# Sixteen row tiles per step from GpSimd in the second layer, in place of fourteen or fifteen from GpSimd and one or two picked by TensorE

## The reference: what is computed

```python
e_feat = jnp.concatenate([x[rol], x[col], edge_attr], axis=-1)
h = jax.nn.relu(e_feat @ W1 + b1)
v = h @ W2 + b2
x_cand = jax.ops.segment_max(v, col, num_segments=num_nodes)
```

```python
x = h[src]; y = h[dst]
c = w_comp[etype]
xb = jnp.einsum('ei,bio->ebo', x, weight)
msg = jnp.einsum('eb,ebo->eo', c, xb)
a = jnp.tanh(jax.nn.relu(jnp.sum(x_hat * y_hat, axis=-1) / scale))
nei = jax.ops.segment_sum(a[:, None] * msg, dst, num_segments=N)
```

## Time and profile before

| | |
|---|---|
| time, median of 3 runs | 4428.0 us (4425.21 to 4429.86) |
| span of the profiled execution | 5626.5 us |
| PE, DVE, ACT, POOL busy in it | 4271.1, 2911.1, 742.0, 3153.8 us |
| granted TensorE clock in it, mean | 0.886 |
| layer 0's steps (copy L885, 104 times) | first at 361.1, last at 2437.9 us |
| layer 1's steps (copy L946, 104 times) | first at 2854.7, last at 5457.4 us |
| DMA bytes | 561.10 MB, mean 100 GB/s |

### The profile page before, as it was taken

How to read it: one execution, slowest core, us unless ns; L and a number is a source line. 1 busy time by engine, 2 the same in 40 slices (tenths; PEclk the granted TensorE clock), 3 DMA queues, 4 the chain that set the end, 5 groups by cost and what they waited for, 6 DMA issues and landing times.

```text
span 5626.5 us, 60937 instructions
## 1 busy us (share of the span) xinstructions
PE 4271.1 (76%) x21573; PEld 1819.3 (32%) x21573; DVE 2911.1 (52%) x5217; ACT 742.0 (13%) x1303; POOL 3153.8 (56%) x3284
## 2 busy tenths in 40 slices
PE   5878888888888777722868888888888878888751
PEld 2434444444444333311323333333323333333211
DVE  5733333333333332334456666666666666666653
ACT  3401111111111100110011111111111111111111
POOL 6556666666666555445455555555555555555535
PEclk8989999999999898965979999999999999999975
DMA  6023323333332222220155556555656555555531
GB/s 262 20 63 86 80 73 81 79 81 77 80 79 73 71 66 66 72 57 25 32 119 132 130 131 134 132 138 130 134 127 139 128 132 127 139 128 135 125 78 30
DMA packets 515150, 561.10 MB, mean 100 GB/s; under 512 B 174276, under 2 KB 371201, under 8 KB 512673
## 3 DMA queue, kind: packets, MB, share of 16 engines
q1 hardware_dynamic: 364960, 392.61, 29.0%
q0 software_dynamic: 104960, 55.52, 6.7%
q10 hardware_dynamic: 44928, 109.07, 5.1%
HBM read 377.15 MB, written 179.68 MB: 99 GB/s over the span
## 4 chain that ended last, share of the span: by engine, by line
PE 41%; another core or an unknown queue 29%; DVE 12%; issue 10%; ACT 3%; DMA 1%; ACTq 1%; DVEq 0%; SPq 0%; POOL 0%; POOLq 0%
PE psum L1471 9%; PE psum L1633 7%; PE psum L1556 6%; PE psum L1565 5%; DVE late L1303 3%; PE psum L1507 3%; PE psum L1517 1%; PE psum L1457 1%; PE psum L1713 1%; PE psum L1447 1%; DVE scan L1316 1%; PE psum L1584 1%; PE psum L1641 1%; PE psum L1596 1%
## 5 line engine op out<-in xcount | busy, mean ns | idle before, releaser
L740 POOL DMA_INDIRECT rows_in<-h_dram,src_idx x1494 | 1428.0, 956 | 1218.2 <-ACT early L941 522.9
L740 POOL DMA_INDIRECT rows_in<-in_x_dram,src_idx x1392 | 1331.1, 956 | 866.0 <-issue 294.7
L1303 DVE TENSOR_TENSOR late<-late,psum 128x512 f32<-128x512 f32 x1664 | 1085.5, 681 | 791.1 <-PE psum L1556 399.7
L1471 PE MATMUL psum<-early,late 128*128 128x448 bf16 x5712 | 1212.6, 367 | 91.6 <-issue 78.3
L1556 PE MATMUL psum<-comp,sel 128*128 128x512 bf16 x1664 | 635.6, 412 | 461.9 <-DVE late L1303 401.4
L1471 PEld LDWEIGHTS psum<-early,late 128*128 128x128 bf16 x5712 | 560.0, 101 | 799.4 <-issue 357.2
L1633 PE MATMUL psum<-x,rows_in 128*128 128x448 bf16 x1988 | 572.1, 358 | 0.0
L1099 DVE TENSOR_TENSOR late<-psum,lane_hot 128x448 f32<-128x448 f32 x272 | 169.3, 622 | 659.9 <-issue 317.2
L1565 PE MATMUL psum<-late,basis 128*32 128x512 f32 x3328 | 493.5, 668 | 0.0
L1556 PEld LDWEIGHTS psum<-comp,sel 128*128 128x128 bf16 x1664 | 160.2, 100 | 969.5 <-DVE late L1303 687.2
L1208 DVE TENSOR_TENSOR_SCAN scan<-fresh,scan,psum 128x512 f32<-128x512 bf16 x103 | 131.8, 1280 | 491.9 <-remote 245.5
(11 more groups left out here) (157 smaller groups left out, 4445.3 us busy)
## 6 DMA issues: line engine op xcount, KB each, us to landing
late<-xs_dram SPq DMA_DIRECT2D x416, 256.0 KB
sp_in<-spread SPq DMA_DIRECT2D x208, 256.0 KB, 2.6
late<-type_dram SPq DMA_DIRECT2D x104, 512.0 KB
sum_rows<-early ACTq DMA_DIRECT2D x104, 512.0 KB
spread<-late SPq DMA_DIRECT2D x16, 1664.0 KB
ea<-in_edge_t SPq DMA_DIRECT2D x104, 256.0 KB
keep<-keep_dram SPq DMA_DIRECT2D x832, 32.0 KB
max_rows<-out ACTq DMA_DIRECT2D x104, 256.0 KB
```

The lines of the kernel that those rows point to most:

```text
L740: pool.indirect_dma_start(out=out, out_offset=None, in_=table, in_offset=bass.IndirectOffsetOnAxis(ap=index, axis=0), engine_sem=pool_issu ...
L1303: dve.tensor_tensor(prod[:, n % G_BUFS, :], x4[:, s.slot(2), g, :], bank[C_BANK[n]][:, :], ALU.mult).then_inc(prod_ready, 1)
L1471: last_ = pe.matmul(hot_bank[tile_slot(s, t)], class_hot[s.slot(2)][:, c, HOT - hot_tiles(s) + t, :], x_parts[:, c, q, :], start=c == 0 an ...
```

## The change

From step 2 of layer 1 on GpSimd gathers all sixteen tiles. `hot1_count` and its tables are gone, and with them TensorE's `hot_rows`, VectorE's `find_lane`, `mask_hot` and `add_hot`, SyncE's `hot_save` in layer 0 and `hot_load` in layer 1 with the DRAM tensor between, and every wait on their semaphores: in `build_hot` (layer 0), ahead of the score sum, `relate`, `source_turn` and the copy of the source rows (layer 1). TensorE's picks in layer 0 and for the first two steps of layer 1 stay as they are.

```diff
-FIRST_HOT1 = 6
-LAST_HOT1 = STEPS - 2
-HOTS1 = (1, 2)
-PIECES1 = {1: (0, 0, 6, 11, 11, 16, 21), 2: (0, 7, 14, 21, 28, 35, 42)}
...
-    return SLOTS - (hot1_count(n) if n >= EARLY1 else min(EARLY_TILES - SLOTS * n, SLOTS))
+    return SLOTS if n >= EARLY1 else SLOTS - min(EARLY_TILES - SLOTS * n, SLOTS)
...
             for n in range(PRE):
-                hot_save(Step(PRE, 0, n))
...
-                if hot(s.plus(2)):
-                    hot_save(s.plus(2))
...
-            for u in range(2):
-                sp.wait_ge(hot_saved[u], 16 * (STEPS // 2))
...
                 keep_load(1, s)
-                if has_pick(s):
-                    hot_load(s)
...
-                for k in range(SLOTS - hot1_count(s.at)):
+                for k in range(SLOTS):
                     if k in (BURST, 2 * BURST, 3 * BURST) and s.at >= 3:
...
-                    wait_count(dve, s, hot_saved[u], s.earlier(2) * 16)
...
-                for t in range(hot1_count(ahead.at)):
-                    mask_hot(ahead, t)
-                product(s, 0)
-                for t in range(hot1_count(ahead.at)):
-                    add_hot(ahead, t)
-                products(s, 1, 5)
+                products(s, 0, 5)
...
-                if has_pick(later):
-                    find_lane(later)
...
-                if has_pick(s):
-                    wait_count(pe, s, hot1_ready, hot1_before(s.at + 1))
...
                 coefs(s, 8, 10)
-                if pick:
-                    hot_rows(later, 0)
                 messages(s, 0)
                 coef(s, 10)
                 messages(s, 1)
-                if pick:
-                    hot_rows(later, 1)
...
                 coef(s, 15)
-                if pick:
-                    hot_rows(later, 5)
                 messages(s, 2)
```

More of the change, by code:

```diff
@@ L204, in build @@
         early_dram = dram("early_dram", [EARLY_TILES * P], fp16)
-        hot_dram = dram("hot_dram", [STEPS * P, max(HOTS1) * CLASSES * P], bf16)
         ident = sb("ident", [P, P])
@@ L282, in build @@
         xs = rows_in[:, 2 * SLOTS * F:2 * SLOTS * F + 2 * LEN].rearrange("p (u n) -> p u n", u=2)
[L283 to L289, removed]
         ea = sb("ea", [P, 2, LEN])
@@ L342, in build @@
         h_low = part(NODE_COLS * F // 2).bitcast(bf16).rearrange("p (c n) -> p c n", c=CLASSES)
-        picks1 = part(max(HOTS1) * PICK * F).rearrange("p (t f h) -> p t f h", f=F, h=PICK)
         h_high = x[:, :, :].rearrange("p t f -> p (t f)").bitcast(bf16).rearrange(
@@ L364, in build @@
         hot_bank = [bank[6 + u][:, 0:PICK * F] for u in range(2)]
-        hot_bank1 = [bank[b][:, 0:PICK * F] for b in (1, 5)]
-        def hot1_bank(s, t):
-            return hot_bank1[t - hot1_count(s.at)]
         lane_v = lane[:, 0:HOT_COLS].rearrange("p (s t) -> p s t", t=HOT)
@@ L457, in build @@
         lane_ready = sem("lane_ready")
-        hot_saved = [sem(f"hot_saved{u}") for u in range(2)]
         h_parts_ready = sem("h_parts_ready")
[L460 to L464, removed]
         early_loaded = [sem(f"early_loaded{u}") for u in range(2)]
@@ L496, in pe_picks @@
             return hot(s) and hot_tiles(s) > 0
-        def has_pick(s):
-            return hot1_count(s.at) > 0
         def gathered1(s, use):
@@ L537, in build @@
         class_v = class_dram.rearrange("(s n) -> s n", s=STEPS)
-        hot_v = hot_dram.rearrange("(s p) n -> s p n", p=P)
         h_nodes = h_dram.rearrange("(p t) f -> p t f", p=P)
@@ L598, in class_load @@
                              class_v[s.at].partition_broadcast(P)).then_inc(classes_in[s.slot(2)], 16)
[L600 to L611, removed]
             def keep_load(n, s):
@@ L937, in src_copy @@
                     wait_count(act, s, gathered[1][s.slot(2)], gathered1(s, 1))
-                if has_pick(s):
-                    wait_count(act, s, hot1_ready, hot1_before(s.at + 1))
                 wait_out(act, s, stored[1])
@@ L1317, in sum_scan @@
                                        ALU.mult, ALU.add).then_inc(scanned[1], 1)
[L1320 to L1339, removed]
             def products(s, a, b):
@@ L1572, in score_sum @@
                 wait_step(pe, s, score_ready)
-                if hot1_count(s.at + 1) == len(hot_bank1):
-                    wait_count(pe, s, hot1_read, hot1_before(s.at + 1) + 1)
                 pe.matmul(bank[1][:, :], ones_blk[:, :], score, start=True, stop=True).then_inc(sum_done, 1)
@@ L1591, in relate @@
                 wait_step(pe, s, query_ready, lag=1)
-                if has_pick(s):
-                    wait_count(pe, s, hot1_read, hot1_before(s.at + 1))
                 for q in range(PARTS):
@@ L1617, in source_turn @@
                 last_.then_inc(x_turned[1], 1)
[L1619 to L1636, removed]
             def find_key(s):
@@ L1647, in step1 @@
             def step1(s):
-                behind, ahead, later = s.plus(-1), s.plus(1), s.plus(2)
-                more, pick = ahead.exists(), has_pick(later)
+                behind, ahead = s.plus(-1), s.plus(1)
+                more = ahead.exists()
                 turns_last = s.known and s.at == STEPS - 2
@@ L1683, in step1 @@
                     find_key(ahead)
-                if pick:
-                    hot_rows(later, 2)
                 coef(s, 13)
-                if pick:
-                    hot_rows(later, 3)
                 coef(s, 14)
-                if pick:
-                    hot_rows(later, 4)
                 coef(s, 15)
-                if pick:
-                    hot_rows(later, 5)
                 messages(s, 2)
```

## The result

| kernel | median us | step of layer 1, us |
|---|---|---|
| before | 4427.3 (4425.21 to 4429.86) | 19.75 |
| changed | 4474.6 (4474.09 to 4482.6) | 20.27 |

The changed kernel is slower by 1.2%: the ratio is 1.0116, with a 95% interval of 1.0103 to 1.0128. The forecast was 4565, with a range of 4420 to 4640: the sign and the new bound were right, the old bound and the size were not, +47 us for +137.

The account below looks back on a forecast made before the run. GpSimd was taken to bound both layers' steps, or very nearly: +178 us for 142 more gathers, -40 us for a loss that goes, everything else nothing, so +138 on 4428.0 us, forecast 4565 us, range 4420 to 4640 us.

Parts of the forecast that it names:

- rival A: Layer 1's steps: GpSimd not quite the bound, real steps 19.3 us before, only +82 us, 4510 us; chance 0.18.
- TensorE's 17.7 us: TensorE's work alone in a layer 1 step before: 12.2 us of chain pieces plus 5.5 us for 1.39 picked tiles.
- The budget of 290 us: Timed 4428.0 us less GpSimd's 4138: 290 left, 246 outside the loops, some 45 for waits in both layers' steps.
- The loss that goes with the change: Layer 1's steps before: GpSimd and TensorE holding each other up, at most 0.8 us a step, 82 us; taken as 40.
- 142 x 1.256 = +178 us: GpSimd in layer 1: 142 more gathered tiles at 1.256 us each, if GpSimd is the bound all along.
- Nothing for VectorE, saves, loads: VectorE's 175 us of masks and sums, 104 saves and 96 loads go: nothing, at most 2.6 us for the transfers.
- The ring, 16.0 to 18.6 us: Source rows' way through DRAM, turn to product 0 to next turn, in layer 1: 16.0 to 18.6 us, below GpSimd's 20.1.
- B: Gap between GpSimd's gathers belongs, at least partly, to the recording: changed kernel faster, -133 us, 4295 us; chance 0.12.
- C: GpSimd still waits for ScalarE's copy or coef 3 each step: steps 20.4 to 21.4 us, 4630 to 4740; chance 0.07.
- D: TensorE's granted clock falls to 0.50 at 61% busy: its step 24.4 us, 440 us above the forecast; chance 0.03.
- The forecast of a span near 5200 us: Changed kernel's profiled span: about 5200 us, 340 to 530 less than the recorded 5626.5, steps at 20.1 to 22 us.
- one sign of being right: In the changed kernel's profile, TensorE idle ahead of the turn of the source rows, released by a gather's DMA.

Follow-up runs that it names:

- undisturbed trace: The kernel before, unchanged, profiled once more: 4427.7 us, span 4425.9 us, layer 1 step 19.75 us.
- b_nomask: The kernel before with mask and lane sum of every picked tile of layer 1 cut from 32 features to 1, matmuls kept: 4422.7 us, ratio 0.9993.
- a_g14: The changed kernel with the gather counts of the kernel before (15 and 14 by turns) and no picks in their place: 4270.1 us, ratio 0.965.
- b_nomm: The kernel before with 2 of the 21 matmuls of every picked tile of layer 1; masks, sums, loads and saves kept: 4270.8 us, ratio 0.9647.
- b_noring: The kernel before with x4 loaded from rows of h already in DRAM, not waiting for the source rows' trip: 4415.1 us, ratio 0.9983.
- b_one: The kernel before with one picked tile in every step from 6 on, in place of one and two by turns: 4330.1 us, ratio 0.9786.
- a_noring: The changed kernel with x4 loaded from rows of h already in DRAM, not waiting for the source rows' trip: 4450.5 us, ratio 1.0061.

## Why the prediction was wrong

The result lies in rival A's range of 4440 to 4530, which had a chance of 0.18, and A's idea holds: GpSimd was not the bound before. A's reason does not. It made TensorE's 17.7 us into 19.3 by a granted clock of 0.92; the step was 19.75 us at a granted clock of 1.00. That the sign came out right hung on half a microsecond a step, 20.27 against 19.75. By the prediction's steps:

**The budget of 290 us: this step failed.** The prediction concluded from it that GpSimd was the bound before. 3280 x 0.30 + 3154 = 4138 us of work for GpSimd is right (3151.7 us busy in the undisturbed trace). But I took the pauses between the loops, 246 us, from the earlier trace rows as if they had that length in a timed run, right after arguing that the recording ran at another pace. Undisturbed the same places have 16.7, under 1, 4.7 and 49.0 us, and 28 follow the last gather: 99 us. The 147 us too much there hid the waits in the loops. I had 45 us left for them in both layers; they were some 190, and about 170 of them lie in layer 1.

**The loss that goes with the change, "at most 0.8 us a step", taken as 40 us: the mis-sized term.** It measured 19.75 - 18.4 = 1.35 us a step, and the waits that vanished are 131 us net. 138 + 40 - 131 = 47: with this one term put right, the sum gives the result; that it does so to the microsecond is luck, for 185 us stand against the 178 and the start and the end gave back 7. The bound of 0.8 had two sources, the budget, and the work of two engines, 17.7 and 18.4 us; and TensorE's 17.7 held no wait of its own. In the undisturbed trace TensorE pauses for VectorE while that runs its two scans. TensorE's pauses in a step whose list has two picks (from 3500), and in one with one pick (from 3521):

```profile
3500.09 0.39 PE L1556 MATMUL psum<-comp,sel 128*128 128x512 bf16 x1 [1.14 <-DVE late L1303]
3521.90 0.39 PE L1556 MATMUL psum<-comp,sel 128*128 128x512 bf16 x1 [1.14 <-DVE late L1303]
3523.67 0.39 PE L1556 MATMUL psum<-comp,sel 128*128 128x512 bf16 x1 [0.39 <-DVE late L1303]
```

Steps with two picks take 21.8 us (from VectorE's scan at 3499.95 to that at 3521.76), those with one 18.3 (to 3540.06): the prediction's 20.1 and 16.2 for TensorE's work and 1.7 and 2.1 us on top, of which these rows show 1.1 and 1.5 as pauses for VectorE. Masks are not the cause of them (b_nomask), and what exactly would remove them was not tried.

**142 x 1.256 = +178 us: nearly right.** Busy and gaps rose by 185 us; a_g14 to the changed kernel, which leaves all else alone, gives 204 us. By GpSimd's groups of the two, 183 us of it are busy time and gaps, and 27 are more waits (45 for 19), which are about the size of the pauses told below (32 us).

**Nothing for VectorE, saves, loads: right.** b_nomm and a_g14 differ by 0.8 us. Layer 0's steps took 1621.8 us before (copies from 289.9 to 1911.7) and 1616.0 after (289.6 to 1905.6), but that isn't the saves: b_noring, b_nomask and b_one have saves and took 1616.5 to 1616.8. It is scatter between executions, and so are most of the 5 us by which the gathers started earlier above.

**The ring, 16.0 to 18.6 us: too short.** On the changed kernel's chain the trips have medians of 5.8 us for xs and 6.0 for x4 (four loads of 256 KB), where I had taken x4 from a single transfer's 2.6 us or twice that, and VectorE waits for x4 in nearly every step (561.4 us in all). Without it (a_noring) only 20 to 24 us go.

**The rivals.** B (the gap of 0.30 us belongs to the recording) is refuted: the gap is 0.30 in traces whose span is the timed length. What B says of before, that TensorE decided, is true. C didn't come: no wait for ScalarE's copy is left. D: TensorE's granted clock fell from 1.00 to 0.89 in layer 1's steps, at 72% busy; no run here shows a cost of it. The forecast of a span near 5200 us was wrong too, 4472.8: of the twelve recordings only the one of the kernel before was longer than its timed runs. And one sign of being right didn't come: TensorE waits for gathers ahead of the turn of the source rows only 0.7 us in the 1800 from 2300 on; SyncE waits for them.

## What to carry to other kernels

When a recorded span is a quarter longer than the timed runs, none of its waits may be used as a length, neither those in the loops nor those between; what may be kept are durations and start-to-start distances of work that waits for nothing. Two engines' sums of work as near to each other as 17.7 and 18.4 us don't tell which one is the bound: add to each the waits that it has for others inside the step before comparing, and where work can be moved between them in small portions, ask for both neighbours of the present split. A chain of waits that runs through DMAs shows a path that fits the pace, not the one that sets it: cutting it gave at most 24 us, thinning the gathers 429.

## What the runs showed that was not expected

In the changed kernel GpSimd stops every 143 us without a wait that the trace shows, 2 to 5 us long, 13 times in layer 1's steps (32 us beyond the usual gaps). Its timeline, three of them:

```profile
2445.05 0.94 POOL L676 DMA_INDIRECT rows_in<-h_dram,src_idx  x1 [2.03 <-issue]
2590.05 0.94 POOL L676 DMA_INDIRECT rows_in<-h_dram,src_idx  x1 [3.87 <-issue]
2732.95 0.94 POOL L676 DMA_INDIRECT rows_in<-h_dram,src_idx  x1 [2.01 <-issue]
```

They are 112 gathers apart each time, seven steps, and a_noring has them at the same gathers. In b_one they are 0.8 us long and 105 gathers apart, again seven steps; in a_g14 they are 0.7 us and 203 gathers, fourteen steps. In these three the distance goes by steps and not by the number of gathers. In the kernel before only one long stop shows (4.93 us at 2327.76); others could lie within its waits. What they are was not tried.

A gather costs 1.25 us from start to start in every trace, 0.94 busy and the gap, except beside one instruction: VectorE's one-hot of 2048 columns (L1170, 0.74 us). In the changed kernel's steps (2300 to 4270 us) all 82 gathers that are busy for 1.0 us or more overlap it, the longest with 1.47 us, and no gather outside it takes more than 0.96. The prediction's "no busy neighbour makes them much longer" holds for the mean, 0.957 us, and not for these.
